# Products of zeros between the sums of a six-pass graph kernel

## What is computed

```python
h = relu(layernorm(x)); x = x + gat(h)          # e = leaky_relu(s_i[dst] + s_j[src]); softmax over dst
h = relu(layernorm(x)); x = x + relational(h)   # segment_sum(proj[src, edge_type], dst) + h @ root + bias
h = relu(layernorm(x)); x = x + gcn_twice(h)    # segment_sum(h[src] * dinv[src] * dinv[dst], dst), twice
h = relu(layernorm(x)); x = x + transformer_twice(h)
# one transformer convolution, 4 heads of 32:
kj, vj = k[src] + e, v[src] + e
alpha = einsum('ehc,ehc->eh', q[dst], kj) / sqrt(32)
w = exp(alpha - amax[dst]) / denom[dst]         # amax, denom: maximum and sum over the edges of dst
out = segment_sum(vj * w, dst) + x @ Ws + bs
```

## Time and profile before

| | us |
|---|---|
| median of 3 runs | 4395.4 |
| the profiled execution | 4429.1 |
| its span | 4427.3 |
| TensorE busy in it | 3005.5 |
| mean granted TensorE clock | 0.809 of full |

### The profile page before, as it was taken

How to read it: one execution, slowest core, us unless ns; L and a number is a source line. 1 busy time by engine, 2 the same in 40 slices (tenths; PEclk the granted TensorE clock), 3 DMA queues, 4 the chain that set the end, 5 groups by cost and what they waited for, 6 DMA issues and landing times.

```text
span 4427.3 us, 55756 instructions
## 1 busy us (share of the span) xinstructions
PE 3005.5 (68%) x16448; PEld 2151.7 (49%) x16708; DVE 2294.8 (52%) x4747; ACT 1768.8 (40%) x4502; POOL 2325.9 (53%) x2401
## 2 busy tenths in 40 slices
PE   3077777883777775877767777546667783676767
PEld 2055555642545553555535555335555562555545
DVE  5033333544666655665545565335555572555557
ACT  2044444543333334333343333234444532444443
POOL 2745555116656606666466665345655634656563
PEclk9986666886888977888879989567777895778787
DMA  4322222132212112222122221345444524455451
GB/s 86 67 56 58 57 60 59 27 124 54 51 46 52 46 41 52 53 52 53 39 73 53 53 54 38 95 127 139 137 136 139 141 62 133 138 139 142 137 147 45
DMA packets 353930, 361.23 MB, mean 82 GB/s; under 512 B 124638, under 2 KB 277413, under 8 KB 353637
## 3 DMA queue, kind: packets, MB, share of 16 engines
q0 software_dynamic: 88064, 208.62, 18.0%
q1 hardware_dynamic: 259430, 147.10, 12.7%
q10 hardware_dynamic: 6148, 1.93, 0.2%
HBM read 327.34 MB, written 30.26 MB: 81 GB/s over the span
## 4 chain that ended last, share of the span: by engine, by line
PE 44%; another core or an unknown queue 16%; DVE 16%; issue 14%; ACT 4%; SPq 3%; DMA 1%; DVEq 1%; ACTq 0%; POOL 0%; POOLq 0%
PE QX L1419 23%; PE NU L1419 12%; PE MTB L1419 7%; DVE sums_transposed L858 3%; DVE extra_sums_transposed L858 2%; SPq L441 2%; DVE gathered_rows L858 2%; DVE messages L858 1%; DVE query_key_products L858 1%; PE MID L1419 1%; ACT gathered_rows L799 1%; DVE scan_scores L1005 1%; DVE messages L1032 1%; DVE gathered_rows L1236 1%
## 5 line engine op out<-in xcount | busy, mean ns | idle before, releaser
L542 POOL DMA_INDIRECT gathered_rows<-key_value_rows,src_index x832 | 831.5, 999 | 648.6 <-DVE messages L858 359.4
L559 POOL DMA_INDIRECT gathered_rows<-gcn_rows,src_index x720 | 687.8, 955 | 508.7 <-issue 195.2
L858 DVE TENSOR_TENSOR sums_transposed<-sums_transposed,NU 128x512 f32 x624 | 424.6, 680 | 982.1 <-remote 521.2
L799 ACT ACTIVATE gathered_rows<-iota_window,dst_in_window_by_edge 128x128 f32<-128x128 f32 x1248 | 397.5, 389 | 721.0 <-remote 490.4
L542 POOL DMA_INDIRECT gathered_rows<-gat_rows,src_index x416 | 398.2, 957 | 407.7 <-DVE messages L1032 208.5
L1419 PE MATMUL NU<-edge_node_onehot,messages 128*128 128x128 f32 x2496 | 425.2, 319 | 79.6 <-issue 69.2
L559 POOL DMA_INDIRECT gathered_rows<-relation_rows,src_relation_index x368 | 348.4, 947 | 235.2 <-issue 95.1
L1419 PEld LDWEIGHTS NU<-edge_node_onehot,messages 128*128 128x128 f32 x2496 | 417.9, 234 | 89.7 <-issue 68.5
L739 ACT ACTIVATE edge_node_onehot<-iota_window,dst_in_window_by_edge 128x128 f32<-128x128 f32 x1248 | 394.9, 387 | 156.4 <-remote 142.9
L1419 PE MATMUL NU<-gathered_rows 128*128 128x128 f32 x2496 | 368.4, 296 | 128.6 <-DVE gathered_rows L1236 49.7
L1419 PE MATMUL QX<-query_window,gathered_rows 128*128 128x384 bf16 x1600 | 346.8, 367 | 141.6 <-DVE gathered_rows L858 98.2
(11 more groups left out here) (310 smaller groups left out, 4925.8 us busy)
## 6 DMA issues: line engine op xcount, KB each, us to landing
query_window<-query_rows SPq DMA_DIRECT2D x832, 66.0 KB
dst_in_window_row<-dst_in_window SPq DMA_DIRECT2D x156, 256.0 KB
gathered_rows<-key_value_rows,src_index POOLq DMA_INDIRECT x832
relation_rows<-gathered_rows SPq DMA_DIRECT2D x25, 512.0 KB
gathered_rows<-gcn_rows,src_index POOLq DMA_INDIRECT x720
dst_in_window_row<-src_place_and_block SPq DMA_DIRECT2D x40, 256.0 KB
gathered_rows<-gat_rows,src_index POOLq DMA_INDIRECT x416
query_window<-gat_target_scores SPq DMA_DIRECT2D x416, 2.0 KB
```

What stands on the lines that cost most here:

```text
L542: pool.indirect_dma_start(out=rows_of(a, s)[:, t, :], out_offset=None, in_=a["table"], in_offset=bass.IndirectOffsetOnAxis(ap=srcI[:, TPG ...
L559: pool.indirect_dma_start(out=linear_rows(p["k"], k)[:, t, :], out_offset=None, in_=p["table"], in_offset=bass.IndirectOffsetOnAxis(ap=p[" ...
L799: last = act.activation(to[:, t, :], iota_j[:], ACT.Square, bias=dstP[:, TPG * k + t:TPG * k + t + 1], scale=-1.0)
L858: return dve.tensor_tensor(o, x, y, op)
```

## The change

Only TensorE's program changes. `keep_busy(bank, n)` is n products of zeros over a whole NU bank, 128x512 in bf16, each a sum by itself that the clear behind it overwrites. In the attention passes `stay_busy(s)` stands at the end of the steps s = 2 to 114: 14 products of zeros in each of the steps 2 to 10, 5 products in each of the steps 11 to 103, none later; from step 11 on it also holds the clear of the next group's NU bank, which stood at the start of `node_sums` behind the wait for `msg_ready`. Where the bank was used before, all of it stands behind a wait for `nu_used`. In the linear passes the clear of the next slot's bank moves to the end of the slot, with its wait for `lin_used`, and 4 products of zeros stand between the two in slots without a pick. In all 3 x (9 x 14 + 93 x 5) + 4 x (55 + 47 + 47) = 2369 products are added.

```diff
+    FILLING, SUMMING, BETWEEN = 14, 6, (5, 5, 5)
...
+            def keep_busy(bank, n):
+
+                for _ in range(n):
+                    mm(bank[:, 0:SPAN], zeros_w[:], fpen[:, 0:TPG, :].rearrange("q c p -> q (c p)"))
...
                     pe.wait_ge(S["msg_ready"], b + s + 1)
-                    clear(NU[s % 2], P)
                     for t in range(TPG):
...
+                def stay_busy(s):
+
+                    g = s + 1 - LAG
+                    if s == 2:
+                        if L3:
+                            pe.wait_ge(S["fin_used"], NBK * (2 + k))
+                        else:
+                            pe.wait_ge(S["idx_ready"], 2)
+                    if g >= 2:
+                        pe.wait_ge(S["nu_used"], b + g - 1)
+                    if g < 0:
+                        keep_busy(NU[g % 2], FILLING)
+                    else:
+                        keep_busy(NU[g % 2], SUMMING - 1 if s < NG else 0)
+                        clear(NU[g % 2], P)
...
+                    if 2 <= s < NG + LAG - 1:
+                        stay_busy(s)
...
                     off = offsets(k, f"lin_off_{p['k']}")
-                    if K >= 2:
-                        pe.wait_ge(S["lin_used"], K - 1)
-                    clear(NU[k % 2], P)
+                    if k == 0:
+                        if K:
+                            pe.wait_ge(S["lin_used"], K - 1)
+                        clear(NU[0], P)
...
+                    if k + 1 < NG:
+                        if K:
+                            pe.wait_ge(S["lin_used"], K)
+                        keep_busy(NU[(k + 1) % 2], 0 if (p["k"], k) in PICK_AT else BETWEEN[p["k"]] - 1)
+                        clear(NU[(k + 1) % 2], P)
```

## The result

The changed kernel takes 4513.8 us (median of 4 runs, 4506.7 to 4523.9) against 4391.4 us for the kernel before beside it: a ratio of 1.0284, 95% interval 1.0250 to 1.0317, so 122 us slower. The prediction had the sign, at 4445 us, and expected 50 us more; its upper end was 4540. The profiled execution of the kernel before, 4429.1 us, was a long one for that kernel, so the two profiled executions are only 83 us apart.

The account below looks back on a forecast made before the run. It took the bound to be a cycle of POOL's unbroken gather runs and late signals. Terms +45 + 15 + 0 + 0 = +60, less 10, gave +50 us: about 4480 profiled, 4445 us on the median, range 4335 to 4540.

Parts of the forecast that it names:

- What bounds the kernel: All passes: signals between engines come late while POOL issues gathers without a pause, so POOL's runs, not TensorE's speed, set the time.
- The price of a product: One product of zeros on TensorE: 0.22 us at full clock, 0.38 to 0.44 us cold.
- Part 1: Attention steps 2 to 10: fillers delay POOL's first messages by 16, 16 and 13 us; +45 us, between +20 and +85.
- Part 2: Last steps of the attention passes, after POOL's last gathers, where TensorE is the bound: +15 us, +5 to +35.
- Part 3: Attention steps with sums while POOL gathers, 33 chunks: half the fillers hidden in waits, the rest paid back; 0 us.
- The bounds of 3 to 4 us a chunk: Steps with sums: most a chunk loses if fillers of four steps go cold on the path; gain up to 4 or 5.
- the signs of being wrong: Mechanism wrong if POOL's runs change length, to 12 or 4 gathers from 8; either way, by more than any term.
- Part 4: Linear slots, 4 products in 149 slots: later sums set against a better clock; 0 us, between -25 and +35.
- The 10 us for a warmer clock: Attention 0 and linear passes: 10 us taken off the +60 because a warmer TensorE clock should give something back.
- Rival 1: Faster: TensorE at full clock at each release, so POOL's restart message comes sooner in all passes; 4340 us, chance 0.25.
- Rival 3: Slower still: fillers run cold and TensorE bounds whole attention chunks, +3 us in 33 chunks; 4544 us, chance 0.15.

## Why the prediction was wrong

*What bounds the kernel: right for the condition in which it was read.* POOL's unbroken runs and the late signals stood in the traces of the kernels beside a kernel before near 4400, and are gone where it takes 3590. One reading is off: the 566 us of attention 0 and the 482 of linear 2 are not whole passes; from the first add to the last they take 645.0 and 520.7 us.

*The price of a product: right.* 3.02 us for 14 is 0.216 each, for 0.22.

*Part 1, first steps: 45 us forecast, 21 measured.* The mechanism held, the size did not. What time the fillers get back was taken at 10 us of idle time and little more in attention 1; the expands, at 1.06 us instead of 1.5 to 2.1, and more idle time gave back a good part besides, and the last block stands behind the softmax. The waits of POOL grew by 8.4 and 7.3 us for 16 and 13, and the shorter first chunk gave some of that back.

*Part 2, tails: 15 us forecast, 17 measured*, from POOL's last gather to the last add (173.2 us in the three passes with moved clears alone, 190.1 with 5 products a step). In the sum of the prediction 13 less 5 is 8, not 7.

*Part 3, steps with sums: 0 forecast, some 62 us measured* (the 79 us of these fillers less 17 for the tails). This is the step that failed. It held that one filler of two lies in time that TensorE would have waited and the other is paid back by the clock, and so put the term at nothing. The experiments contradict both: the fillers cost the same when they are put ahead of the wait that ends the stall, the cost grows with their number from 2 a step on, and products that take hardly any of TensorE's time cost two thirds to four fifths of it. So idle time ahead of the MTB clear was not free space, and neither the product's time nor the clock is the main part of the price; the instructions themselves carry most of it. Why an instruction costs that much while signals are late stays open: late delivery of TensorE's instructions would do it and shows in the traces, but its amount does not follow the cost. The bounds of 3 to 4 us a chunk took in the measured 2 us a chunk (62 us in 33 chunks); nothing in the argument led to it. The run lengths of POOL did change, as named among the signs of being wrong, but that accounts for some 12 us at most.

*Part 4, linear slots: 0 forecast, 18 measured*, all in linear 0, inside the bounds; linear 1 and 2 are at 0.

*The 10 us for a warmer clock* did not show up. By the Trainium skill, "TensorE: Matmul & The Clock Gate", section "Part 1: The HAM clock gate", activity releases the throttle; the trace agrees (0.69 to 0.84 in attention 0), and the time shows that the clock was not what these passes waited for.

*The sum.* 21 + 17 + 62 + 18 - 6 = 112 of the 122 us. The sign came out of parts 1 and 2; the size came from the two terms that were put at 0.

*The rivals.* Rival 1 had the direction of the clock right (to 0.84 and 0.89, not to full) and the time wrong. Rival 3 has the nearer number (4544 us), but its mechanism is not what happened: the clock rose, and no attention pass came near to being filled by TensorE (512 of 650 us in attention 2); that its number is near is luck.

## What to carry to other kernels

Idle time of an engine is not room for work if what ends it is another engine's pattern: change one number of the filler (how many, how wide, where) before trusting a sum of hidden and exposed time. Here, where one engine's long run of indirect DMAs made everybody's signals late, added instructions had a price even when their work was next to nothing, and a higher clock bought nothing on a path that waited for signals. Where the same engine never waited, nearly all of the added work was free. Before a gain or loss of a few per cent is put down to an edit, the kernel before belongs beside it in the same runs: here it moved by 18% between sets of runs.

## What was not expected of the hardware

- With the same kernel the chip is in one of two conditions: signals, SyncE's DMA issues and, it seems, TensorE's instructions come late while POOL issues indirect DMAs without a break (4371 to 4457 us), or they do not (3579 to 3601 us). The changed kernel was traced in both, at 4510 and 3622 us. The gathers of attention 0 take about 0.95 us each, 1.25 with the gap, in both. What decides between them is not known; the records name chip 15 for a set of runs of each kind.
- In the late condition eight DMA issues of SyncE take 22.4 us during a long run of gathers and 3.95 us outside it.
- In it, too, 5 products of 16 columns a step cost 1.1%, and 5 of 512 columns 1.4 to 1.6%. Without late signals the whole change, with products in the first steps and in the linear passes besides, costs 0.9%.
- A pause of 1.8 us on POOL after every 4 gathers made the kernel 2.95% faster in the late condition, with the gain in the stretches where a ring is filled.
